# Turning the second layer's expert weights in beats 1 to 4 instead of ahead of the first score

## The chip, the cores and the metric

The kernel runs on one core of one Trainium2 chip. The metric is the device time of one execution in microseconds (us). The engines are TensorE (PE in the profile, with PEld for its weight loads), VectorE (DVE), ScalarE (ACT), GpSimd (POOL) and SyncE (SP), which here issues nearly all the transfers.

## The reference

The input x is 8 sequences of 512 tokens with 128 features. Everything is float32.

```
x = x + attention(layernorm(x))      # 16 heads of 8 features; Q, K, V and output projections 128x128, with biases
u = layernorm(x)
logits = u @ Wr.T + br               # 8 experts, the best 2 of each token, gates by softmax of the two
h = relu(u @ W1[e].T + b1[e])        # W1: 8 x 512 x 128
o = h @ W2[e].T + b2[e]              # W2: 8 x 128 x 512
x = x + layernorm_affine(u + sum over the 2 experts of gate * o)
```

## The kernel before

The work is in two blocks: attention with routing, then the experts. In the attention block each engine runs its own in-order program, and the programs are written as a loop over **beats** T, unrolled when the kernel is built, from -18 to 150. There are 16 beats per sequence (4 quads of heads times 4 tiles of 128 query tokens) and 8 sequences. A semaphore wait stands wherever one engine needs another's result.

In a beat T from 0 to 127, PE makes four score matmuls (`scores`, L810, one per head of a quad), each into one of three banks of `s_psum`, and DVE reduces each to a row maximum (`maxima`, L643). The score of number k (four per beat) waits until the reduction of number k-3 has freed its bank. Six beats later the same scores are made transposed (`scores_t`, L826), with the maximum added by rows of `qs` that the SHIFT task has brought in (mneg turned by PE at L848, copied by ACT at L512, sent by a DMA at L346). ACT takes their exponential into `pt` (L546), and two beats after that PE multiplies with the values (L896).

Between these, `early_tasks` places side tasks that share one bank, `side_psum`, and so one order. For sequence 0 the inputs are prepared in beats below 0. For sequence 1 they are: in beat 2 XT (four transposes of the normed input, L856, copied by ACT at L530), in beat 3 K and in beat 6 Q (a projection each, two instructions at L858; ACT takes the rounded part at L518, DVE the rest at L650, SP stores both to DRAM at L323). SHIFT of quad 0 is in beat 4. The first transposed score is in beat 6.

SP issues in beat -6 all loads of K and Q parts of sequence 0 (L334, L339), then the inputs of sequences 2 to 7 (L363).

The **expert weights** are 16 blocks of 128x512: eight of W1, eight of W2. They are loaded into `pt` (which the exponentials use only from beat 6 on; the program calls them w1raw and w2raw). A block is turned by four PE transposes (L929) into a bank of `st_psum`, block n into bank n mod 3. ACT copies it out (L589), rounded into `w1h` for W1, whole into `w2t` for W2. For W1, DVE also writes the remainder `w1l` (L714). PE waits before block n until block n-3 is copied, and before the very first transposed score until all 16 are (`if k == 0`). `expert_weights(T)` says which blocks belong to beat T. It is called at the end of the beat on PE, ACT and DVE.

Of the kernel before, what the change touches and what calls it, by code (L numbers as in the profile page):

```python
# [35 lines left out]
E = 8  # L36
# [81 lines left out]

def expert_weights(T):

    return range(2 * (T + 8), 2 * (T + 8) + 2) if -8 <= T < 0 else ()


def tiles(b, j=0, count=TILES):
# [44 lines left out]
def attention(nc, x, Wq, bq, Wk, bk, Wv, bv, Wo, bo, Wr, br, W1, b1, W2, beta, kept, sent, parts):  # L169
    xres, ident, fill = kept.xres, kept.ident, kept.fill  # L170
    with ExitStack() as ctx:
# [328 lines left out]
        def _(act):  # L500
# [31 lines left out]
            def beat(T):  # L532
# [51 lines left out]
                for n in expert_weights(T):  # L584
                    act.wait_ge(turned, n + 1)
                    src = weights_bank(n).rearrange("p (c d) -> p c d", c=FC)
                    dst = kept.w1h if n < E else kept.w2t
                    at = FC * (n % E)
                    nc.scalar.copy(dst[:, at:at + FC, :], src).then_inc(w_high, 1)  # L589
# [13 lines left out]
        def _(dve):  # L603
# [75 lines left out]
            def beat(T):  # L679
# [30 lines left out]
                for n in expert_weights(T):  # L710
                    if n < E:
                        dve.wait_ge(w_high, n + 1)
                        at = slice(FC * n, FC * n + FC)
                        nc.vector.tensor_tensor(kept.w1l[:, at, :], weights_bank(n).rearrange("p (c d) -> p c d", c=FC),  # L714
                                                kept.w1h[:, at, :].bitcast(F32), ALU.subtract).then_inc(w_low, 1)
# [65 lines left out]
        def _(pe):  # L781
# [118 lines left out]
            def beat(T):  # L900
# [18 lines left out]
                for n in expert_weights(T):  # L919
                    if n == 0:  # L920
                        pe.wait_ge(cols_ready, 1)
                    if n % E == 0:
                        pe.wait_ge((w1_loaded, w2_loaded)[n // E], 16)
                    if n >= ST_BANKS:
                        pe.wait_ge(w_high, n - ST_BANKS + 1)
                        pe.wait_ge(w_low, min(n - ST_BANKS + 1, E))
                    for c in range(FC):
                        src = w1raw[:, FC * n + c, :] if n < E else w2raw[:, n - E, P * c:P * c + P]
                        ins = nc.tensor.transpose(weights_bank(n)[:, P * c:P * c + P], src, ident[:])  # L929
                    ins.then_inc(turned, 1)  # L930
# [315 lines left out]
```

## Time and profile before

| | us |
|---|---|
| median of 3 runs | 753.96 |
| lowest, highest | 751.37, 755.16 |
| profiled execution | 752.29 |
| its span | 750.5 |
| PE busy | 609.3 (81%) |
| DVE busy | 489.0 (65%) |
| ACT busy | 447.4 (60%) |
| POOL busy | 242.6 (32%) |

The span is the profiled stretch of the program; 1.8 us of the execution's time lie around it. The attention block fills the time to about 530 us, the experts most of the rest. The change touches what lies between 29 and 56 us. TensorE runs at one of two clocks, 1.2 or 2.4 GHz; the profile's column of the granted clock gives it as 0.50 or 1.00. Before the first recorded switch that column reads 1.00 whatever the clock is, so there the durations of like instructions tell it.

### The profile page before, as it was taken

The page shows a single profiled execution, that of the slowest core. Times are in us where ns is not written, and L with a number is a line of the kernel's source. Part 1 is how long each engine was busy: PE and PEld are TensorE (multiplying, and loading weights), DVE is VectorE, ACT ScalarE, POOL GpSimd, SP SyncE. Part 2 cuts the span into 40 slices and gives each one's busy share as a digit, 9 for nine tenths or more (in the row PEclk, how much of TensorE's full clock was granted, in tenths as well). Part 3 has the DMA queues.
Part 4 walks back from the last instruction along what each step waited for, and adds up shares of the span by engine and source line. Part 5 has one row for each costly group of instructions (what it writes and reads, how often), then busy time and mean ns, then how long its engine had stood idle before and what let it go on. Part 6 is the DMA issues. An engine that isn't in the chain of part 4 may idle for free. (4 is left out here: it accounts for less than half of the span.)

```text
span 750.5 us, 13269 instructions
## 1 busy us (share of the span) xinstructions
PE 609.3 (81%) x3750; PEld 321.2 (43%) x3750; DVE 489.0 (65%) x1319; ACT 447.4 (60%) x945; POOL 242.6 (32%) x454
## 2 busy tenths in 40 slices
PE   2899999879988997987987998995229998999680
PEld 1633333323333432332332333332128988888530
DVE  3579989968967985985995887751204444444357
ACT  2718888867956965875885786683114444544333
POOL 5200101150240332214115005016425665555534
PEclk9959999989998998998998899899559999999976
DMA  7552122122122122022112211000121221221193
GB/s 219 195 153 66 44 69 83 49 67 74 37 85 72 33 84 84 26 65 89 49 47 70 65 45 48 6 0 30 50 83 54 65 66 56 69 66 57 47 238 98
DMA packets 54216, 54.47 MB, mean 73 GB/s; under 512 B 8286, under 2 KB 37514, under 8 KB 54164
## 3 DMA queue, kind: packets, MB, share of 16 engines
q1 hardware_dynamic: 48372, 44.19, 20.8%
q0 software_dynamic: 4416, 8.53, 3.2%
q10 hardware_dynamic: 1376, 1.13, 0.5%
q8 instruction: 24, 0.39, 0.2%
q14 instruction: 28, 0.23, 0.1%
HBM read 29.01 MB, written 24.81 MB: 72 GB/s over the span
## 5 line engine op out<-in xcount | busy, mean ns | idle before, releaser
L643 DVE TENSOR_REDUCE mneg<-s_psum 128x1 f32<-128x512 f32 x512 | 325.9, 684 | 89.5 <-PE s_psum L810 55.7
L546 ACT ACTIVATE pt<-st_psum 128x512 f32<-128x512 f32 x512 | 279.9, 598 | 93.3 <-PE st_psum L826 82.7
L826 PE MATMUL st_psum<-qs,ks 64*128 64x512 f32 x512 | 202.5, 471 | 24.8 <-ACT pt L546 19.4
L810 PE MATMUL s_psum<-ks,qs 64*128 64x512 f32 x512 | 208.3, 482 | 3.3 <-DVE mneg L643 2.1
L896 PE MATMUL pv_psum<-pt,vst 128*16 128x512 f32 x1024 | 142.8, 632 | 0.0
L810 PEld LDWEIGHTS s_psum<-ks,qs 64*128 64x128 f32 x512 | 84.4, 196 | 120.2 <-DVE mneg L643 94.9
L826 PEld LDWEIGHTS st_psum<-qs,ks 64*128 64x128 f32 x512 | 82.4, 193 | 69.1 <-ACT pt L546 52.7
L1099 ACT ACTIVATE hid<-h_psum,b1c 128x256 f32<-128x256 f32 x144 | 57.2, 474 | 71.2 <-PE h_psum L1204 69.3
L1062 POOL DMA_INDIRECT results<-res,goal_now x72 | 71.6, 994 | 33.7 <-issue 33.7
L1211 PE MATMUL y_psum<-w2t,hid 128*128 128x128 f32 x576 | 73.1, 280 | 0.0
L1211 PEld LDWEIGHTS y_psum<-w2t,hid 128*128 128x128 f32 x576 | 68.9, 194 | 0.9 <-issue 0.2
L490 POOL DMA_INDIRECT sent<-xrow,placeu x64 | 62.3, 973 | 18.4 <-issue 18.4
L1144 DVE COPY goal_now<-goals 128x1 uint32 x72 | 11.1, 154 | 64.2 <-DMA results<-res,goal_now 57.1
L461 POOL TENSOR_TENSOR vareps<-moments,eps 128x4 f32<-128x4 f32 x8 | 1.6, 200 | 149.2 <-DVE moments L726 149.1
L1202 PE MATMUL h_psum<-xh,w1h 128*128 128x256 f32 x144 | 44.0, 306 | 2.5 <-DVE xl L1120 2.3
L1190 PE MATMUL x_psum<-ident,lot 128*128 128x128 f32 x74 | 16.5, 306 | 33.2 <-DMA lot<-sent 33.1
L1204 PE MATMUL h_psum<-xh,w1l 128*128 128x256 f32 x144 | 41.0, 285 | 0.0
L1203 PE MATMUL h_psum<-xl,w1h 128*128 128x256 f32 x144 | 41.0, 285 | 0.0
L896 PEld LDWEIGHTS pv_psum<-pt,vst 128*16 128x16 f32 x1024 | 17.0, 95 | 39.3 <-ACT pt L546 22.6
L538 ACT COPY pvs<-pv_psum 128x512 f32<-128x512 f32 x32 | 18.8, 589 | 25.1 <-remote 14.4
L1091 ACT CAST xh<-x_psum 128x256 fp32r<-128x256 f32 x37 | 13.9, 376 | 33.1 <-PE x_psum L1190 32.3
L428 POOL TENSOR_TENSOR start<-fill,zero_e 128x8 f32<-128x8 f32 x8 | 1.6, 204 | 89.0 <-DVE counts L691 89.0
(164 smaller groups left out, 711.3 us busy)
## 6 DMA issues: line engine op xcount, KB each, us to landing
parts<-high SPq DMA_DIRECT2D x32, 256.0 KB, 3.0
ks<-parts SPq DMA_DIRECT2D x128, 48.0 KB
qs<-parts SPq DMA_DIRECT2D x128, 48.0 KB
lot<-sent SPq DMA_DIRECT2D x37, 132.0 KB
parts<-low SPq DMA_DIRECT2D x16, 256.0 KB, 3.1
got<-results SPq DMA_DIRECT2D x16, 256.0 KB, 5.1
xres<-in_L_attn_x_dram SPq DMA_DIRECT2D x8, 256.0 KB, 3.6
pt<-in_L_ffn_W_dram SPq DMA_DIRECT2D x1, 2048.0 KB, 14.5
```

What stands on the lines that cost most here:

```text
L490: nc.gpsimd.indirect_dma_start(out=sent, out_offset=bass.IndirectOffsetOnAxis(ap=placeu[:, j, k:k + 1], axis=0), in_=xrow[:, k, j, :], in_ ...
L546: nc.scalar.activation(pt[:, n % PT_SLOTS, (g + 2) % 4, :], st_psum[:, k % ST_BANKS, :], ACT.Exp, scale=SCALE).then_inc(exp_done, 1)
L643: nc.vector.tensor_reduce(mneg[:, (n // 4) % 2, at:at + 1], s_psum[:, k % S_BANKS, :], AX_X, ALU.max, negate=True).then_inc(max_done, 1)
L810: mm(s_psum[:, k % S_BANKS, :], qs[rows, c, P * (n % 4):P * (n % 4) + P], ks[rows, c, g, :], start=True, stop=True).then_inc(s_made, 1)
L826: mm(st_psum[:, k % ST_BANKS, :], ks[rows, c, g, P * (n % 4):P * (n % 4) + P], qs[rows, c, :], start=True, stop=True).then_inc(st_made, 1)
L896: ins = mm(pv_psum[32 * g:32 * g + 16, 0, :], vst[:, b % 2, n % 4, 4 * (q % QUADS) + g, :], pt[:, n % PT_SLOTS, g, :], start=(n % 4 == 0), ...
L1062: nc.gpsimd.indirect_dma_start(out=results, out_offset=bass.IndirectOffsetOnAxis(ap=goal_now[:, h:h + 1], axis=0), in_=res[:, h, :], in_of ...
L1099: nc.scalar.activation(hid[:, f, :], h_psum[:, f, 0:SLOTS], ACT.Relu, bias=b1c[:, FC * e + f:FC * e + f + 1]).then_inc(relu_act, 1)
L1202: mm(dst, w1h[:, k, :], xh[:], start=True, stop=False)
L1203: mm(dst, w1h[:, k, :], xl[:], start=False, stop=False)
L1204: mm(dst, w1l[:, k, :], xh[:], start=False, stop=True).then_inc(h_made, 1)
L1211: ins = mm(y_psum[:, h, 0:D], hid[:, f, P * h:P * h + P], w2t[:, FC * e + f, :], start=(f == 0), stop=(f == FC - 1))
```

## The change

One function is changed. The eight blocks of W1 stay in beats -8 to -5, two each. The eight blocks of W2 move from beats -4 to -1 into beats 1 to 4, two each, on PE and on ACT. On DVE nothing moves, since it has no work for W2.

```diff
 def expert_weights(T):
 
-    return range(2 * (T + 8), 2 * (T + 8) + 2) if -8 <= T < 0 else ()
+    if -8 <= T < -4:
+        return range(2 * (T + 8), 2 * (T + 8) + 2)
+    return range(E + 2 * (T - 1), E + 2 * (T - 1) + 2) if 1 <= T < 5 else ()
```

The lines below the change stand two lines lower in the changed file (L929 is L931 there, L810 is L812, and so on). On PE, the place from the last blocks of W1 to the first transposed score, before the change:

```order
L929 MATMUL st_psum<-ident,pt 128x128 [waits w_low,w_high]
L929 MATMUL st_psum<-ident,pt 128x128 x3
L810 MATMUL s_psum<-ks,qs 128x512 [waits kq_in0]
L810 MATMUL s_psum<-ks,qs 128x512 x2
L810 MATMUL s_psum<-ks,qs 128x512 [waits max_done] x7
L856 MATMUL side_psum<-ident,xn 128x128 [waits xn_done,side_done]
L856 MATMUL side_psum<-ident,xn 128x128 x3
L810 MATMUL s_psum<-ks,qs 128x512 [waits max_done] x4
L858 MATMUL side_psum<-xt,wt 128x512 [waits side_done]
L810 MATMUL s_psum<-ks,qs 128x512 [waits max_done] x2
```

And the beginning of the same place after it (beats 0 to 3):

```order
L812 MATMUL s_psum<-ks,qs 128x512 [waits kq_in0]
L812 MATMUL s_psum<-ks,qs 128x512 x2
L812 MATMUL s_psum<-ks,qs 128x512 [waits max_done] x5
L931 MATMUL st_psum<-ident,pt 128x128 [waits w_low,w_high,w2_loaded]
L931 MATMUL st_psum<-ident,pt 128x128 x3
L931 MATMUL st_psum<-ident,pt 128x128 [waits w_low,w_high]
L931 MATMUL st_psum<-ident,pt 128x128 x3
L812 MATMUL s_psum<-ks,qs 128x512 [waits max_done] x2
L858 MATMUL side_psum<-ident,xn 128x128 [waits xn_done,side_done]
L858 MATMUL side_psum<-ident,xn 128x128 x3
L812 MATMUL s_psum<-ks,qs 128x512 [waits max_done] x2
```

The 32 transposes of W2 no longer stand ahead of the first score; eight of them follow the fourth score of each of the beats 1 to 4. On ACT, before:

```order
L589 CAST w1h<-st_psum 128x512 [waits turned] x8
L589 COPY w2t<-st_psum 128x512 [waits turned] x8
L564 ACTIVATE xn<-xres,shift,rstd 128x128 [waits shift_done]
L564 ACTIVATE xn<-xres,shift,rstd 128x128 x3
L530 COPY xt<-side_psum 128x512 [waits side_made]
L518 ACTIVATE high<-side_psum,bcols 128x512 [waits k_stored,side_made]
L512 CAST shift_rows<-side_psum 16x128 [waits side_made]
```

and after:

```order
L591 CAST w1h<-st_psum 128x512 [waits turned] x8
L566 ACTIVATE xn<-xres,shift,rstd 128x128 [waits shift_done]
L566 ACTIVATE xn<-xres,shift,rstd 128x128 x3
L591 COPY w2t<-st_psum 128x512 [waits turned] x2
L532 COPY xt<-side_psum 128x512 [waits side_made]
L591 COPY w2t<-st_psum 128x512 [waits turned] x2
L520 ACTIVATE high<-side_psum,bcols 128x512 [waits k_stored,side_made]
L591 COPY w2t<-st_psum 128x512 [waits turned] x2
L514 CAST shift_rows<-side_psum 16x128 [waits side_made]
L591 COPY w2t<-st_psum 128x512 [waits turned] x2
```

The eight copies now stand in pairs around the copies of XT, K and SHIFT, and the norm of sequence 1 is no longer behind them.

## Rows read from the trace of the kernel before

**Rows 1.** PE in order of time (start, duration, instruction, idle before), beats -8 to 6.

```profile
22.30 2.82 PE L929 MATMUL st_psum<-ident,pt 128*128 128x128 f32 x12 [0.53 <-DVE wrt L634]
25.36 4.06 PE L929 MATMUL st_psum<-ident,pt 128*128 128x128 f32 x20 [0.24 <-DVE w1l L714]
29.65 4.20 PE L929 MATMUL st_psum<-ident,pt 128*128 128x128 f32 x32 [0.23 <-DVE w1l L714]
33.78 0.73 PE L810 MATMUL s_psum<-ks,qs 64*128 64x512 f32 x3
...
39.37 1.11 PE L856 MATMUL side_psum<-ident,xn 128*128 128x128 f32 x4
...
42.71 2.07 PE L858 MATMUL side_psum<-xt,wt 128*128 128x512 f32 x2
...
51.93 0.79 PE L826 MATMUL st_psum<-qs,ks 64*128 64x512 f32 x1
...
53.08 2.07 PE L858 MATMUL side_psum<-xt,wt 128*128 128x512 f32 x2
```

**Rows 2.** DVE in order of time, from the last remainders of W1 to beat 6.

```profile
30.69 0.86 DVE L608 BATCH_NORM_STATS2 stats<-xres 128x6 f32<-128x128 f32 x4
31.59 0.38 DVE L613 BATCH_NORM_AGGREGATE moments<-stats 128x2 f32<-128x6 f32 x4
34.31 6.07 DVE L643 TENSOR_REDUCE mneg<-s_psum 128x1 f32<-128x512 f32 x10 [2.35 <-PE s_psum L810]
41.24 2.48 DVE L643 TENSOR_REDUCE mneg<-s_psum 128x1 f32<-128x512 f32 x4 [0.86 <-PE s_psum L810]
45.54 1.29 DVE L643 TENSOR_REDUCE mneg<-s_psum 128x1 f32<-128x512 f32 x2 [1.82 <-PE s_psum L810]
46.75 0.74 DVE L650 SCALAR_TENSOR_TENSOR low<-side_psum,bcols,high 128x512 fp32r<-128x512 f32 x1
47.41 6.15 DVE L643 TENSOR_REDUCE mneg<-s_psum 128x1 f32<-128x512 f32 x10
55.91 1.29 DVE L643 TENSOR_REDUCE mneg<-s_psum 128x1 f32<-128x512 f32 x2 [2.36 <-PE s_psum L810]
```

**Rows 3.** Stretches: length, busy us (count) of PE, PEld, DVE, ACT, POOL, granted clock, DMA share, GB/s.

```profile
38.00:38.50 0.50, 0.45 (x1) 0.18 (x1) 0.50 (x1) 0.00 (x0) 0.00 (x0) 1.00 0.32 98
38.50:39.00 0.50, 0.40 (x2) 0.28 (x1) 0.50 (x2) 0.00 (x0) 0.00 (x0) 0.60 0.37 127
...
46.50:47.00 0.50, 0.50 (x1) 0.07 (x1) 0.50 (x2) 0.00 (x0) 0.00 (x0) 0.50 1.31 313
47.00:47.50 0.50, 0.08 (x1) 0.00 (x0) 0.50 (x2) 0.00 (x0) 0.00 (x0) 0.50 0.43 103
...
48.50:49.00 0.50, 0.50 (x3) 0.27 (x1) 0.50 (x2) 0.00 (x0) 0.00 (x0) 0.50 0.43 98
...
51.00:51.50 0.50, 0.50 (x2) 0.28 (x1) 0.50 (x2) 0.00 (x0) 0.00 (x0) 0.50 0.57 205
51.50:52.00 0.50, 0.50 (x3) 0.07 (x3) 0.50 (x2) 0.00 (x0) 0.00 (x0) 0.50 0.00 0
...
55.50:56.00 0.50, 0.50 (x6) 0.27 (x4) 0.09 (x1) 0.12 (x1) 0.00 (x0) 0.83 0.00 0
```

**Rows 4.** L929's transposes, 22 to 27.5 us: duration ns min/median/max, first and last start.

```profile
L929 PE MATMUL st_psum<-ident,pt x22: 421/421/476, 22.3 to 27.3; 128*128 128x128 f32 x22
```

**Rows 5.** L929's transposes from 29 to 34 us.

```profile
L929 PE MATMUL st_psum<-ident,pt x36: 272/273/328, 28.8 to 33.6; 128*128 128x128 f32 x36
```

**Rows 6.** SP's issues in order of time.

```profile
24.73 1.67 SPq L339 DMA_DIRECT2D ks<-parts  x4
26.51 1.52 SPq L339 DMA_DIRECT2D qs<-parts  x4
...
40.38 3.29 SPq L363 DMA_DIRECT2D xres<-in_L_attn_x_dram  x6
```

**Rows 7.** Transfers of the first 60 us: size, median us from issue to landing.

```profile
parts<-high SPq DMA_DIRECT2D x6, 256.0 KB, 3.3
...
xn<-in_L_ffn_b_dram SPq DMA_DIRECT2D x1, 16.0 KB, 2.4
```

**Rows 8.** PE in order of time, a later projection in the fast clock.

```profile
91.47 0.50 PE L826 MATMUL st_psum<-qs,ks 64*128 64x512 f32 x1
...
92.13 1.13 PE L858 MATMUL side_psum<-xt,wt 128*128 128x512 f32 x2
93.19 0.50 PE L810 MATMUL s_psum<-ks,qs 64*128 64x512 f32 x1
```

**Rows 9.** Groups by line, 34 to 56 us: busy us, mean ns, idle before, released by.

```profile
L643 DVE TENSOR_REDUCE mneg<-s_psum 128x1 f32<-128x512 f32 x27 | 16.7, 681 | 7.4 <-PE s_psum L810 7.4
...
L826 PEld LDWEIGHTS st_psum<-qs,ks 64*128 64x128 f32 x5 | 1.2, 285 | 1.9 <-issue 1.5 <-DMA qs<-shift_rows 0.4
```

**Rows 10.** DVE after that projection.

```profile
93.76 1.29 DVE L643 TENSOR_REDUCE mneg<-s_psum 128x1 f32<-128x512 f32 x2 [0.47 <-PE s_psum L810]
```

## The prediction

> **What bounds the kernel now.** I read the page first, then PE, DVE, ACT and SP in order of time over the first 80 us, then the granted clock in short stretches. The page says that the attention block keeps PE, DVE and ACT all busy. The change moves no work out of the kernel, so it can only gain where an engine that sets the pace stands idle, and lose where it adds to that engine's line. Those places lie between 29 and 56 us. From beat 7 on the beats follow one another by events alone; nothing there is tied to a fixed time, so I take a lead that is won by then as kept to the end.
>
> The reader should see three things. First, PE turns W2 from 29.65 to 33.8 us and makes the first score at 33.78 [rows 1], while DVE has finished all it had to do at 31.97 and waits 2.35 us for that score [rows 2]. Here the moved work stands on the path. Second, from the first reduction to beat 6 DVE goes on without a pause except in three places: 0.86 us behind XT, 1.82 us behind the K projection, 2.36 us behind the Q projection and the first transposed score [rows 2]. Third, TensorE is in the slow clock for the last two: it fell at about 38.6 and rose at about 55.7 us [rows 3]. The transposes tell that it was also slow at the start: they took 421 ns up to 27.3 us and 273 ns from 28.8 us on [rows 4, 5].
>
> I follow the lead of the changed kernel, the time by which the same reduction on DVE starts earlier than before. Reductions are counted from 0, four per beat, 0.607 us each (6.07 / 10 [rows 2]).
>
> **Removed: the wait ahead of the first score.** DVE's work up to 31.97 is unchanged. PE has the last W1 block done at about 29.4 (25.36 + 4.06 [rows 1]). The first score then needs the first loads of K and Q. Their last issue ends at 28.03 (26.51 + 1.52 [rows 6]). The trace has no landing for them; a smaller transfer landed 2.4 us after its issue and a larger one 3.3 us [rows 7], so they are there between 30.4 and 31.3. With the 0.53 us from a first score's start to its reduction (34.31 - 33.78), DVE could start between 30.9 and 31.9. Both ends are before 31.97, so DVE's own work decides: a lead of 34.31 - 31.97 = 2.34 us. The cover at the late end is only 0.1 us. If the loads come 1 us later than that, the lead is 0.9 us less.
>
> **Moved: eight transposes into each of beats 1 to 4.** In the fast clock 32 of them take 4.20 us, 0.131 each; in the slow clock the first twelve take 2.82 us, or (2.82 - 0.42) / 11 = 0.218 each [rows 1, 4]. Two blocks cost PE 1.05 us fast or 1.75 us slow. What hides them is the supply of three filled banks, 1.8 us of reductions, less the time to make the next score (0.5 fast, 0.8 slow). The fast case fits in; the slow one does not, by about 1 us. So the clock decides the rest.
>
> Before, the clock fell after PE had gone over from dense transposes to scores alone, paced by DVE at 0.61 us. In the changed kernel that stretch starts at about 30 instead of 33.8, so I take the clock as slow by beat 1. Then: score 7 waits for reduction 4 to end, at 31.97 + 5 x 0.607 = 35.0; with its 0.45 us the transposes run from 35.5 to 37.25. Score 8 is ready 0.79 us later, at 38.0. DVE ran dry at 36.8. Before, reduction 8 started at 34.31 + 8 x 0.607 = 39.2, so the lead is 1.2 us. XT follows score 9 at 38.1 and takes 1.11 us, and reduction 10 starts at 39.9 against 41.24 [rows 2]: lead 1.3.
>
> From 35.0 on PE has no pause at all: score, transposes, two scores, XT, two scores, and beat 2's transposes (40.0 to 41.75). I take it that this brings the fast clock back at about 42, before the K projection. What speaks for it is the start: between 22.3 and 27.3 us PE did nothing but these transposes, and by 28.8 it was fast [rows 1, 4, 5]. The Trainium skill, in "TensorE: Matmul & The Clock Gate", section "Part 4: PE-mode transpose", says the contrary, that transposes do not engage the full clock and do not count as busy in the same way. The trace differs, 421 ns and then 273 ns with only transposes between. By the page the clock would stay low through beats 1 to 4, which is the last rival below.
>
> With the fast clock the K projection takes 1.13 us [rows 8] for 2.07 [rows 1]. It runs from about 42.5 to 43.6, reduction 14 starts at 44.05 (45.54 before), the K remainder ends at 45.95 and reduction 16 starts there (47.41 before): lead 1.5. The transposes of beats 3 and 4 take 1.05 us each behind three filled banks and cost nothing. If that cover is gone they cost what rival 3 and 4 give.
>
> **The copies on ACT.** Two copies a beat, 1.1 us, where ACT is otherwise nearly idle up to beat 6. Behind them stand the XT copy, the K part and the SHIFT copy. Beat 1's pair ends at 37.9 and XT is made at 39.2, so nothing waits. Beat 2's pair ends at about 42.4, before the K projection does. The norm of sequence 1 comes about 1 us earlier on ACT. All of this I cost at nothing, at most 0.3 us. The wait of the first transposed score for all 16 blocks is met at least 3 us before.
>
> **Beat 6.** The first transposed score waits for the SHIFT rows, a transfer that SP issues behind the three stores of K. From the end of the K remainder (47.41) to that score (51.93) it was 4.5 us [rows 1, 2], and the score's last wait was for those rows [rows 9]. So it comes at 45.95 + 4.5 = 50.4, and the lead is still 1.5. From it to reduction 26 it was 55.91 - 51.93 = 3.98 us, of which 2.07 are the Q projection in the slow clock. In the fast clock the same pieces are 0.66 from a transposed score to the projection and 1.63 from the projection to the reduction behind it (92.13 - 91.47 and 93.76 - 92.13 [rows 8, 10]), together 2.3. Reduction 26 starts at 52.7 for 55.91: lead 3.2. This is the sum: 2.3 won at the start, 0.8 lost net up to beat 4, 1.7 won at Q. Against the profiled execution it gives 752.29 - 3.2 = 749.1, against the median 753.96 - 3.2 = 750.8. The profiled execution lies low in the three runs, so I weight the median more and say **750.5**.
>
> **Rivals.**
>
> 1. *The clock stays or comes back sooner.* If it is fast before the beat 2 transposes, or never falls, the K remainder would end 0.9 to 1.8 us sooner still. But then something else is late: the six input loads, issued from 40.38 on, keep the DMA engines full until 47.0 [rows 3, 6], and the stores of K and the SHIFT rows stand behind them. The stores' data moved from about 48.5 to 51.4 [rows 3]. The first transposed score is then at about 49.9, a lead of 2.0, and with 1.7 at Q it is 3.7 to 4.0: about 750.1 to 750.3 on the median, 748.5 on the profiled execution. For it: XT and transposes are dense work. Against it: PE's sparse scores are longer alone at the start. The Trainium skill, "DMA: Bandwidth & Descriptors", section "Queues, rings and completion order", says that a ring's descriptors are consumed in order, which is the reason for this queueing; no row here separates the rings.
> 2. *The clock comes back late*, in beat 3 or 4, behind the K projection. Before, one K projection at 42.7 did not bring it back, though PE was busy [rows 1, 3]. Then the lead at K is about 0.1 us (39.9 + 2.8 to the projection's start, against 42.71), 0 to 0.3 at the first transposed score, and 1.7 from Q: 1.9 us, 752.1 on the median.
> 3. *The lead is lost at the start or later*: the first loads come late (up to 1 us), or a later stretch of slow clock moves against it. The gain is then 0 to 2 us, 753.
> 4. *The slow clock lasts through beats 1 to 5 (slower).* Then PE sets the pace. K runs 42.6 to 44.7 as before, two blocks of transposes from 45.4 to 47.2 make reduction 16 start at 47.9 (47.41 before), beat 4's run from 49.4 to 51.1, score 20 is ready at 51.8 when DVE ran dry at 50.4, and the first transposed score stands behind five scores at 53.4 instead of 51.93: 1.5 us later, and no gain at Q. The time would be 755.5 on the median, 753.8 on the profiled execution. It decides from the point where two or more of the four pairs are turned in the slow clock behind the K projection. Against it: PE would have no pause at all in all these beats.
>
> **Numbers.** Forecast 0.42, rival 1 0.23, rival 2 0.17, rival 3 0.10, rival 4 0.08. The three runs are spread by 3.8 us, 0.5%, which is about what can be told from no change. A gain over 0.5% is 3.77 us; only rival 1 reaches it, and the forecast by the scatter of medians: 0.34 in all. Slower by over 0.5% needs rival 4 and scatter: 0.05. The rest, 0.61, is the same. The range from 747.0 to 754.6 holds rivals 1 to 3 with 2 us of scatter; the forecast alone would be 748.5 to 752.
>
> **What would show it.** DVE's first reduction at 32.0, not 34.3 (if later, the loads). Transposes of beat 1 at 421 ns and of beats 3 and 4 at 273 ns; the clock slow from about 35 and fast again before the K projection, which then takes 1.1 us. The K remainder ends near 46, the first transposed score is near 50.4, its idle time still put down to the SHIFT rows, reduction 26 near 52.7. The total of DVE's idle time up to there falls from 7.4 us [rows 9] to about 4. I am wrong if K or Q still takes 2.07 us, if the first transposed score comes after 51.9, or if the lead at beat 7 is not found again in the last reduction of the attention block.

## The result and the profile after

The changed kernel is slower by about half a percent, which is small but clear of the scatter: a median of 757.26 us over 18 runs (749.83 to 759.10) against 751.76 us over 18 runs of the kernel before (748.38 to 755.19), ratio 1.0052 with a 95% interval of 1.0033 to 1.0071 (the two medians alone give 1.0073). The profiled execution took 756.26 us with a span of 754.5 (750.5 before). The forecast was 750.5, from a lead of 3.2 us. The range ended at 754.6, so the time lies outside it.

The ratios leave out executions over 1.5% above the fastest of the same kernel; for two kernels below that removes many, so their medians over all executions are given too.

The beginning came as forecast. DVE in order of time (start, duration, instruction, idle before it), which answers to [rows 2]:

```profile
31.45 4.84 DVE L645 TENSOR_REDUCE mneg<-s_psum 128x1 f32<-128x512 f32 x8
37.99 1.29 DVE L645 TENSOR_REDUCE mneg<-s_psum 128x1 f32<-128x512 f32 x2 [1.71 <-PE s_psum L812]
40.19 1.29 DVE L645 TENSOR_REDUCE mneg<-s_psum 128x1 f32<-128x512 f32 x2 [0.91 <-PE s_psum L812]
43.23 1.29 DVE L645 TENSOR_REDUCE mneg<-s_psum 128x1 f32<-128x512 f32 x2 [1.76 <-PE s_psum L812]
46.39 1.29 DVE L645 TENSOR_REDUCE mneg<-s_psum 128x1 f32<-128x512 f32 x2 [1.86 <-PE s_psum L812]
...
53.95 3.68 DVE L645 TENSOR_REDUCE mneg<-s_psum 128x1 f32<-128x512 f32 x6 [1.76 <-PE s_psum L812]
59.48 1.29 DVE L645 TENSOR_REDUCE mneg<-s_psum 128x1 f32<-128x512 f32 x2 [1.86 <-PE s_psum L812]
```

The first reduction starts at 31.45 instead of 34.31, with no wait in front of it: a lead of 2.9 us. Reduction 8 is at 37.99 (38.0 forecast), reduction 10 at 40.19 (39.9). Then the lead goes. Reduction 12 is at 43.23, reduction 14 at 46.39 against 45.54 before, and reduction 26 at 59.48 against 55.91: 3.6 us late.

PE in order of time, which answers to [rows 1], shows why:

```profile
29.51 0.73 PE L812 MATMUL s_psum<-ks,qs 64*128 64x512 f32 x3 [0.52 <-DMA qs<-parts]
32.16 3.18 PE L812 MATMUL s_psum<-ks,qs 64*128 64x512 f32 x5 [1.92 <-DVE mneg L645]
35.27 1.97 PE L931 MATMUL st_psum<-ident,pt 128*128 128x128 f32 x8
37.16 1.22 PE L812 MATMUL s_psum<-ks,qs 64*128 64x512 f32 x2
38.31 1.12 PE L858 MATMUL side_psum<-ident,xn 128*128 128x128 f32 x4
...
40.51 1.97 PE L931 MATMUL st_psum<-ident,pt 128*128 128x128 f32 x8
42.41 1.22 PE L812 MATMUL s_psum<-ks,qs 64*128 64x512 f32 x2
43.55 2.07 PE L860 MATMUL side_psum<-xt,wt 128*128 128x512 f32 x2
...
55.39 0.76 PE L828 MATMUL st_psum<-qs,ks 64*128 64x512 f32 x1
```

The loads were there at 29.5. All four pairs of blocks take 1.97 us, and K, and later Q, take 2.07. From 35.27 to 54.3 us PE has no idle time at all: PE sets the pace and DVE waits. The next idle time, 0.36 us, stands ahead of a score at 54.69. The granted clock, by stretch (columns as in [rows 3]):

```profile
30.00:32.00 2.00, 0.24 (x3) 0.00 (x0) 1.97 (x10) 0.00 (x0) 0.31 (x2) 1.00 0.44 123
32.00:34.00 2.00, 1.75 (x4) 0.80 (x4) 2.00 (x5) 0.64 (x2) 1.25 (x3) 0.68 0.26 82
34.00:60.00 26.00, 25.64 (x70) 13.85 (x69) 14.87 (x24) 8.93 (x18) 1.27 (x1) 0.50 0.44 125
60.00:62.00 2.00, 1.22 (x8) 0.70 (x6) 2.00 (x5) 2.00 (x5) 0.00 (x0) 1.00 0.00 0
```

PE was idle for nearly two microseconds from 30.24 on, since it had made three scores and DVE freed the first bank only at 32.1. PE went on at 32.16, and the clock fell within the next stretch, at about 32.7 (0.68 in the mean), and stayed at 1.2 GHz for all of 34 to 60 us, though PE was busy for 25.64 of these 26. Before, it was slow from 38.6 to 55.7 [rows 3]. The totals by line from 29 to 61 us (columns as in [rows 9]) say the same: DVE's reductions waited 11.1 us for PE's scores (7.4 before, in the stretch of [rows 9]), and the 32 transposes average 426 ns.

```profile
L645 DVE TENSOR_REDUCE mneg<-s_psum 128x1 f32<-128x512 f32 x28 | 17.5, 681 | 11.1 <-PE s_psum L812 11.1
...
L931 PE MATMUL st_psum<-ident,pt 128*128 128x128 f32 x32 | 7.9, 426 | 0.0
```

Compared at the same instruction of later batches, the profiled execution stays 3.6 to 5.0 us late to the end of the attention block, and ends 4.0 us late.

### The profile page after: what moved, and what is told of

The parts are those of the page before. It is cut to its first block and busy times, and to the rows that moved or that the text cites. A ratio compares the mean times of both kernels' runs of the same rounds, so it can differ in the third digit from the quotient of the medians.

```text
span 754.5 us, 13269 instructions
## 1 busy us (share of the span) xinstructions
PE 612.5 (81%) x3750; PEld 323.2 (43%) x3750; DVE 488.8 (65%) x1319; ACT 447.6 (59%) x945; POOL 242.3 (32%) x454
## 3 DMA queue, kind: packets, MB, share of 16 engines
q10 hardware_dynamic: 1376, 1.13, 0.5%
## 5 line engine op out<-in xcount | busy, mean ns | idle before, releaser
L812 PE MATMUL s_psum<-ks,qs 64*128 64x512 f32 x512 | 209.5, 484 | 4.1 <-DVE mneg L645 2.7
L812 PEld LDWEIGHTS s_psum<-ks,qs 64*128 64x128 f32 x512 | 84.9, 198 | 120.1 <-DVE mneg L645 90.3
L1146 DVE COPY goal_now<-goals 128x1 uint32 x72 | 11.1, 154 | 63.3 <-DMA results<-res,goal_now 52.7
L1192 PE MATMUL x_psum<-ident,lot 128*128 128x128 f32 x74 | 16.6, 307 | 33.9 <-DMA lot<-sent 33.4
L1093 ACT CAST xh<-x_psum 128x256 fp32r<-128x256 f32 x37 | 13.8, 374 | 33.7 <-PE x_psum L1192 32.6
```

Of the source, the lines that this page charges most:

```text
L812: mm(s_psum[:, k % S_BANKS, :], qs[rows, c, P * (n % 4):P * (n % 4) + P], ks[rows, c, g, :], start=True, stop=True).then_inc(s_made, 1)
```

## The experiments

Each kernel is the changed one or the one before, as said, with the edit shown; "..." marks lines left out. Each was timed beside the kernel before, whose median was 753.28, 747.87 or 747.55 us in the three sets, so a kernel is compared within its own set. A gain is called shown only where the interval of the ratio stays below 1 and the median over all executions agrees. "Reduction 26" is the first one behind the Q projection in beat 6: at 55.91 us before and at 59.48 in the changed kernel.

**The transposes left out.** Changed kernel; the result lacks W2's turned form.

```diff
-                    act.wait_ge(turned, n + 1)
+                    act.wait_ge(turned, min(n + 1, E))
...
+                    if n >= E:
+                        continue
                     if n == 0:
                         pe.wait_ge(cols_ready, 1)
```

> The changed kernel with the 32 PE transposes of W2 left out (ACT's eight copies stay and copy what is in the banks, so W2's turned form is not computed). Theory A (the transposes in beats 1 to 4, all in the slow clock, are the whole loss): the first reduction stays at about 31.5 us, the clock still falls at about 33 and stays low through K and Q, and reduction 26 starts at 52.8 to 53.5 us instead of 59.5 (before 55.9); the time is 2.5 to 3 us under before, ratio 0.996 to 0.997. Theory B (the early start itself costs, by loads or stores that come into each other's way): reduction 26 comes at 55 or later, ratio 0.999 to 1.002.

Measured: 752.10 us against 753.28, ratio 0.9982 (0.9959 to 1.0004). Reduction 26 starts at 54.15, a lead of 1.8. The clock fell at 31.8, in the same idle time, and rose at 55.7. So the early start is real, and the transposes in the slow clock are the difference of 5.3 us at reduction 26. The forecast of 52.8 to 53.5 was too early: the first transposed score waited 0.6 us for the SHIFT rows, and the first reduction came at 31.85. For the whole execution no gain is shown, since the interval holds 1; see the end of this section.

**Ordinary matmuls against the identity in place of the transposes of W2.** Changed kernel.

```diff
-                        ins = nc.tensor.transpose(weights_bank(n)[:, P * c:P * c + P], src, ident[:])
+                        if n < E:
+                            ins = nc.tensor.transpose(weights_bank(n)[:, P * c:P * c + P], src, ident[:])
+                        else:
+                            ins = mm(weights_bank(n)[:, P * c:P * c + P], src, ident[:], start=True, stop=True)
```

> The changed kernel with the eight W2 blocks of beats 1 to 4 turned by ordinary matmuls against the identity instead of transposes: same count and shape, but more array time each (an ordinary 128x128 one has about twice the passes of a transpose). Theory A with the page's rule (transposes do not hold or bring the fast clock, ordinary matmuls do): the clock rises in beat 1, 2 or 3, before 46 us; K then takes 1.1 us and reduction 26 starts at 54 to 57.5, ratio 0.998 to 1.003, in spite of the dearer instruction. Theory C (the kind of instruction is the same to the clock, it stays low because PE's work in these beats is too thin): the pairs cost about 3.4 us each in the slow clock, reduction 26 starts at 64 or later, ratio 1.010 or more.

Measured: 753.44 us against 753.28, ratio 1.0015 (0.9983 to 1.0046). PE in order of time:

```profile
35.52 3.78 PE L934 MATMUL st_psum<-ident,pt 128*128 128x128 f32 x16
...
42.57 3.78 PE L934 MATMUL st_psum<-ident,pt 128*128 128x128 f32 x16
46.28 1.21 PE L812 MATMUL s_psum<-ks,qs 64*128 64x512 f32 x2
47.42 1.12 PE L860 MATMUL side_psum<-xt,wt 128*128 128x512 f32 x2
48.48 0.73 PE L812 MATMUL s_psum<-ks,qs 64*128 64x512 f32 x2
49.14 2.05 PE L934 MATMUL st_psum<-ident,pt 128*128 128x128 f32 x16
```

A pair of blocks is now 16 instructions instead of 8 and takes 3.78 us instead of 1.97 in the slow clock, yet the clock came back at 47.4 us, in the place where with transposes it did not for 13 us more. It came later than expected (46), and reduction 26 is at 59.33, later than expected (54 to 57.5), as the two dear pairs had been paid by then. Ordinary matmuls do here what the transposes did not. They also keep the array busy twice as long, so kind and amount aren't told apart by this run.

**Four blocks ahead, one in each of beats 1 to 4.** All by transposes. The edit is written against the changed kernel.

```diff
-    if -8 <= T < -4:
+    if -8 <= T < -2:
         return range(2 * (T + 8), 2 * (T + 8) + 2)
-    return range(E + 2 * (T - 1), E + 2 * (T - 1) + 2) if 1 <= T < 5 else ()
+    return range(12 + (T - 1), 13 + (T - 1)) if 1 <= T < 5 else ()
```

> Four W2 blocks ahead of the first score (beats -4 and -3), one in each of beats 1 to 4. PE stood idle for about 2 us between the first scores in the changed kernel, so both theories expect the first reduction at 31.5 to 32.0. Theory A: the four blocks left cost 0.9 us each in the slow clock, mostly hidden (three banks give 1.8 us less 0.8); reduction 26 starts at 54 to 56, ratio 0.997 to 1.000. Theory B: no gain over before, 1.000 to 1.003.

Measured: 750.72 us against 753.28, ratio 0.9973 (0.9949 to 0.9997). The first reduction is at 31.76 (31.45 in the changed kernel) after a wait of 0.48 us for its score, so four blocks ahead cost at most half a microsecond: they fill most of the time in which PE would have waited for the loads and for DVE. The clock fell at 35.7, in beat 1. From the end of the transposes at 31.3 PE made scores alone, with no idle time over 0.55 us, and the four transposes of beat 1 had begun only at 35.33. Reduction 26 is at 55.80, level with the kernel before, so the 0.3% of the whole time did not come from these beats.

**The clock held in the kernel before by an added projection.** Its result is not read.

```diff
+                if 0 <= T < 6:
+                    pe.wait_ge(w_high, 2 * E)
+                    mm(st_psum[:, 1, :], wt[:, 0, :], xt[:, 0], start=True, stop=True)
```

> The kernel before with one more ordinary 128x128 by 128x512 projection at the end of each of beats 0 to 5, whose result nothing reads. It measures what the slow clock of 38.6 to 55.7 us costs the kernel before. If ordinary matmuls hold the fast clock (theory A with the page's rule): the clock does not fall before beat 7, the added projections take 1.1 us each and are hidden, K and Q take 1.13 instead of 2.07, reduction 26 starts at 52.5 to 54 instead of 55.9, ratio 0.996 to 0.998. If the clock falls all the same (theory C): the added ones take 2.07 us each, PE sets the pace, reduction 26 starts at 61 or later, ratio 1.006 or more.

Measured: 749.08 us against 753.28, ratio 0.9936 (0.9907 to 0.9966). More work and a shorter time. PE's stretch, and DVE at Q:

```profile
34.00:60.00 26.00, 23.12 (x83) 9.60 (x83) 22.86 (x38) 9.81 (x22) 1.27 (x1) 1.00 0.43 124
```

```profile
53.71 1.29 DVE L643 TENSOR_REDUCE mneg<-s_psum 128x1 f32<-128x512 f32 x2 [1.03 <-PE s_psum L810]
```

The clock does not fall from 34 to 60 us (granted 1.00). Between the first reduction and reduction 26 DVE waits 3.0 us in all, where it waited 5.0 (0.86, 1.82 and 2.36 us in [rows 2]). Reduction 26 is 2.2 us earlier; 0.67 us of that was there at the first reduction (33.64 against 34.31), ahead of all added work. So the slow clock costs the kernel before about 2 us up to this point, and the twin that follows, whose first reduction is level, gives the cleaner number.

**The same with eight transposes in place of the projection.** The twin of the last, in the kernel before.

```diff
+                if 0 <= T < 6:
+                    pe.wait_ge(w_high, 2 * E)
+                    for i in range(8):
+                        nc.tensor.transpose(st_psum[:, 1, P * (i % 4):P * (i % 4) + P], xt[:, 0, P * (i % 4):P * (i % 4) + P],
+                                            ident[:])
```

> The kernel before with eight more transposes at the end of each of beats 0 to 5 (about the time of one projection in the fast clock), whose result nothing reads. It is the twin of the run that added one projection there and kept the fast clock. If transposes do not count for the clock: it falls between 35 and 39 us as before, the added ones then take 1.75 to 2.0 us a beat, and reduction 26 starts at 60 to 63 us; ratio 1.004 to 1.010. If any dense work counts: the clock stays fast, reduction 26 starts at 53.5 to 54, ratio 0.993 to 0.998.

Measured: 744.48 us against 747.87, ratio 0.9953 (0.9922 to 0.9984). The 48 added transposes, by duration (ns min/median/max), and the clock over 38 to 56 us:

```profile
L921 PE MATMUL st_psum<-ident,xt x48: 272/273/331, 35.5 to 51.0; 128*128 128x128 f32 x48
```

```profile
38.00:56.00 18.00, 16.34 (x80) 9.31 (x80) 15.74 (x26) 4.94 (x10) 0.00 (x0) 1.00 0.54 159
```

The clock does not fall with transposes either. The first reduction is at 34.30, as before, and reduction 26 at 53.71, so the whole lead of 2.2 us comes from the stretch between. That both twins have reduction 26 at 53.71 is in part chance: the projections' kernel started 0.67 us earlier, and then waited 0.24 us for the SHIFT rows, which PE used at 51.4 us in both.

**64 transposes without a pause ahead of the first score.** Kernel before; one execution.

```diff
+                if T == -1:
+                    pe.wait_ge(w_high, 2 * E - 2)
+                    for i in range(64):
+                        nc.tensor.transpose(...)
```

> The kernel before with 64 more transposes, without a pause, ahead of the first score (8.4 us in the fast clock). In the kernel before, the clock rose at about 28 us with only transposes since 22.3, which speaks against the rule that transposes do not count. If dense transposes hold the clock: they all take about 273 ns, the clock falls only after they end at about 42. If they do not: it falls amid them, before 39 us, and the rest take 421 ns. The first reduction comes at 42 to 46 us and the time is 8 to 12 us longer either way.

Measured: 753.70 us, one execution, 5.8 us over the median of the kernel before where 8 to 12 was expected; the 64 transposes took 7.2 us and not 8.4, and the first reduction came at 40.79, ahead of the 42 to 46 expected. All 64 took 272 to 326 ns. The clock fell at 46.1 us, nearly 6 us after they ended, with scores and, just ahead of the fall, the four transposes of XT in between, and no idle time over 0.55 us. The Trainium skill, in "TensorE: Matmul & The Clock Gate", section "Part 4: PE-mode transpose", has it that transposes do not engage the full clock. These two runs disagree for an array that is already fast. In the slow clock of the changed kernel, eight transposes a beat among scores did not bring it back, which agrees; at the start of the kernel before it rose with transposes alone [rows 4, 5], which does not.

**The changed kernel with the clock held.** Two projections in the gap of beat 0, half of one in each of beats 1 to 4, one in beat 5; the transposes where the change has them.

```diff
+                if T == 0:
+                    pe.wait_ge(side_done, SIDE["Q", 0] + 1)
+                    for _ in range(2):
+                        mm(side_psum[:, 0, :], wt[:, 0, :], xt[:, 0], start=True, stop=True)
                 scores(T, 3)
...
+                if 1 <= T < 6:
...
+                    cols = 256 if T < 5 else 512
+                    mm(st_psum[:, (n0 - 1) % ST_BANKS, 0:cols], wt[:, 0, :], xt[:, 0, 0:cols], start=True, stop=True)
```

> The changed kernel with the clock held by ordinary matmuls whose results nothing reads: two projections between the third and fourth score of beat 0, where PE stood idle, half a projection in each of beats 1 to 4, one in beat 5. The W2 transposes stay where the change put them. Theory A (the slow clock, not the place, made the move dear): the clock stays fast, each pair of blocks takes 1.05 us, PE has about 2.9 us of work a beat for 2.43 of DVE, and reduction 26 starts at 52.5 to 54.5 instead of 59.5; ratio 0.991 to 0.997. Theory P (the place costs in either clock, by waits on the copies or by the order behind the scores): reduction 26 at 57 or later, ratio 1.000 or more.

Measured: 747.10 us against 747.87, ratio 0.9981 (0.9954 to 1.0007). Each pair took 1.04 us, K 1.12, and the K remainder ended at 44.1, a lead of 3.4 over the kernel before. But the first transposed score started at 51.88 and had waited 1.67 us for the SHIFT rows. The clock fell soon after this wait, at 53.3, and reduction 26 came at 54.72, just behind the 54.5 expected. For the whole execution no gain over the kernel before is shown.

**Only the gap of beat 0 filled.** Changed kernel with the first of these two edits alone.

```diff
+                if T == 0:
+                    pe.wait_ge(side_done, SIDE["Q", 0] + 1)
+                    for _ in range(2):
+                        mm(side_psum[:, 0, :], wt[:, 0, :], xt[:, 0], start=True, stop=True)
                 scores(T, 3)
```

> The changed kernel with one edit: two projections whose result nothing reads stand between the third and fourth score of beat 0, where PE was idle for 1.9 us. Nothing is added in beats 1 to 6. Theory D, formed from the runs so far: transposes do hold the fast clock, but do not bring it back when the array is in the slow one; the changed kernel loses because the clock falls in the gap that the change opens ahead of beat 1. Then here the clock stays fast at least through beats 1 to 4, the four pairs take 1.05 us each, K takes 1.1, and reduction 26 starts at 52.5 to 55 instead of 59.5; ratio to before 0.993 to 0.999. Against it, theory E (transposes amid scores do not hold it, the added work of the other run in beats 1 to 4 did): the clock falls before 42 us and reduction 26 is at 57 or later, ratio 1.001 or more.

Measured: 746.97 us against 747.55, ratio 0.9979 (0.9941 to 1.0017). PE in order of time, and the clock:

```profile
30.13 1.98 PE L915 MATMUL side_psum<-xt,wt 128*128 128x512 f32 x4
32.61 2.89 PE L812 MATMUL s_psum<-ks,qs 64*128 64x512 f32 x5 [0.49 <-DVE mneg L645]
35.43 1.09 PE L935 MATMUL st_psum<-ident,pt 128*128 128x128 f32 x8
...
40.05 1.12 PE L860 MATMUL side_psum<-xt,wt 128*128 128x512 f32 x2
...
50.63 0.49 PE L828 MATMUL st_psum<-qs,ks 64*128 64x512 f32 x1 [2.58 <-DMA qs<-shift_rows]
```

```profile
32.50:47.00 14.50, 13.44 (x60) 7.51 (x60) 13.19 (x23) 7.47 (x15) 2.48 (x4) 1.00 0.59 165
```

This is the run that names the cause. Nothing was added in beats 1 to 6, and yet the clock stayed fast, every pair took 1.09 us, and reduction 26 moved from 59.48 to 54.19. The clock fell only at 51.2, after PE's wait of 2.58 us for the SHIFT rows, so Q still took 2.08. The change lost because the clock was slow from ahead of beat 1 on, and two projections in the gap are enough to prevent it. Against the changed kernel, timed in the same set, the medians are 746.97 and 751.55 us; against the kernel before no gain is shown.

What this run does not tell apart is the idle time from the lack of dense work, for the two projections end both. In the changed kernel 6.3 us lie between the last transpose of W1 (29.0) and the first of W2 (35.27), with scores alone and 1.92 us of idle time. In three kernels without such idle time the clock fell all the same, 4.4 to 5.8 us after the last dense transposes: 31.3 to 35.7 with four blocks ahead, 33.9 to 38.6 before, 40.3 to 46.1 with 64 transposes. So it may well have fallen ahead of beat 1 without the idle time too. No run leaves the gap out and keeps the scores alone.

**The gap filled with work that is needed.** Four blocks ahead, two in beat 0, two in beat 1; nothing added.

```diff
-    if -8 <= T < -4:
+    if -8 <= T < -2:
         return range(2 * (T + 8), 2 * (T + 8) + 2)
-    return range(E + 2 * (T - 1), E + 2 * (T - 1) + 2) if 1 <= T < 5 else ()
+    return range(12 + 2 * T, 14 + 2 * T) if 0 <= T < 2 else ()
```

> No added work: four W2 blocks ahead of the first score, two at the end of beat 0, two at the end of beat 1, all by transposes. It fills the gap of beat 0 with work that has to be done anyway. Theory D: first reduction at 31.7, all transposes in the fast clock (1.05 us a pair), the clock falls later, at 38 to 42 us when scores are alone, as in the kernel before; K and Q take 2.07 and reduction 26 starts at 53 to 54; ratio 0.995 to 0.998. Theory E: the clock falls at about 35 as in the run with half moved, reduction 26 at 55 to 56, ratio 0.997 to 1.000.

Measured: ratio 0.9947 (0.9906 to 0.9988), from 8 of 12 executions; over all of them the median is 747.73 against 747.55, so no gain is shown. In its trace, of an execution of 750.00 us, the first reduction is at 31.75, the pairs take 1.1 us, and the K projection is still fast (39.63, 1.13 us); the clock fell at 45.7, later than the 38 to 42 expected, amid scores alone. The first transposed score is at 50.11 after 2.51 us of wait for the SHIFT rows, and reduction 26 at 54.12, a lead of 1.8.

**Both edits together.** Four blocks ahead by transposes; one block in each of beats 1 to 4 by ordinary matmuls; one unread projection in beats 0 and 5.

```diff
-    if -8 <= T < -4:
+    if -8 <= T < -2:
...
+    return range(12 + (T - 1), 13 + (T - 1)) if 1 <= T < 5 else ()
...
+                        if n < E + 4:
...
+                            ins = mm(weights_bank(n)[:, P * c:P * c + P], src, ident[:], start=True, stop=True)
...
+                if T in (0, 5):
+                    pe.wait_ge(w_high, 12 if T == 0 else 2 * E)
+                    mm(st_psum[:, 2 if T == 0 else 0, :], wt[:, 0, :], xt[:, 0], start=True, stop=True)
```

> Made from the two edits that paid: four W2 blocks turned by transposes ahead of the first score, where PE has nothing else; the other four one per beat in beats 1 to 4, turned by ordinary matmuls against the identity; and one projection with an unread result in beats 0 and 5. Theory A with the rule on transposes: the clock does not fall before beat 7, the first reduction starts at 31.5 to 31.9 and reduction 26 at 51.5 to 52.8, against 53.7 with the projections alone and 55.8 with the half move alone; ratio to before 0.989 to 0.994. Theory C: one ordinary block a beat is too thin, the clock falls at 35 to 38 and reduction 26 is at 55 to 58, ratio 0.998 to 1.003.

Measured: 742.77 us against 747.87, ratio 0.9924 (0.9892 to 0.9957). The K remainder ended at 43.9, but the first transposed score:

```profile
51.68 0.49 PE L828 MATMUL st_psum<-qs,ks 64*128 64x512 f32 x1 [2.37 <-DMA qs<-shift_rows]
```

It is hardly earlier than the 51.93 of [rows 1]. The clock fell at 52.8, after this wait, where it was expected to hold to beat 7, and reduction 26 is at 54.76, where 51.5 to 52.8 was expected. The gain over the kernel before is shown, but at 5.1 us of the medians it is larger than the lead of 1.15 us at reduction 26.

**The input loads issued behind the SHIFT rows.** The last kernel with one edit on SP: the loads of sequences 2 to 7 and of beta move from beat -6 to beat 5.

```diff
+                if T == 5:
                     for b in range(2, B):
                         sp.dma_start(xres[:, TILES * b:TILES * b + TILES, :], x_tiles[:, b]).then_inc(x_loaded, 16)
...
```

> The version with half ahead, ordinary matmuls and two projections, and on SP one edit: the six input loads and beta are issued in beat 5 instead of beat -6. There the first transposed score stood at 51.7 us and waited 2.4 us for the SHIFT rows, although the K remainder had ended at 43.9. If the wait is due to those loads ahead in the queue, the first transposed score comes at 48.5 to 49.5 and reduction 26 at 50.5 to 51.5, 2 to 4 us earlier than there; ratio to before 0.987 to 0.991. If it is the issue and the latency of SHIFT's own transfer, nothing changes: 0.991 to 0.994.

Measured: ratio 0.9845 (0.9790 to 0.9900), from 5 of 12 executions; over all, 742.56 us against 747.55, or 0.993. PE and DVE:

```profile
49.21 0.50 PE L829 MATMUL st_psum<-qs,ks 64*128 64x512 f32 x1
```

```profile
51.49 1.29 DVE L646 TENSOR_REDUCE mneg<-s_psum 128x1 f32<-128x512 f32 x2 [0.46 <-PE s_psum L813]
```

The score comes 2.5 us earlier and waits for nothing, and reduction 26 is 4.4 us ahead of the kernel before. So the loads held the SHIFT rows up. They did it in two ways, as SP's issues show, first with the loads ahead of the stores and then with the loads behind SHIFT:

```profile
41.37 3.40 SPq L365 DMA_DIRECT2D xres<-in_L_attn_x_dram  x6
44.81 0.51 SPq L366 DMA_DIRECT2D beta<-in_L_ffn_beta_dram  x1
45.78 1.22 SPq L325 DMA_DIRECT2D parts<-high  x2
...
47.69 0.60 SPq L348 DMA_DIRECT2D qs<-shift_rows  x1
```

```profile
44.30 1.22 SPq L325 DMA_DIRECT2D parts<-high  x2
...
46.22 0.60 SPq L348 DMA_DIRECT2D qs<-shift_rows  x1
```

With the loads ahead, SP was still issuing them and beta when the K remainder ended at 43.9, and the SHIFT rows were issued 3.8 us after that; with the loads behind, 1.9 us after it (44.3 to 46.22). That part, 1.9 us, is SP's own time. The rest is the transfer: 3.4 us from the end of SHIFT's issue to the score that waited for it (48.29 to 51.68), at most 2.4 with the loads behind (46.82 to 49.21).

This version beats the kernel before, by 5 us of the medians. It is not shown to be faster than the version it was made from: 742.56 us here and 742.77 there, in spite of 3.3 us more of lead at reduction 26.

**The changed kernel again**, for a second trace.

> The changed kernel itself once more, for a second trace. Its times spread from 750 to 759 us, so the clock may not take the same course in every execution. Theory D: in an execution near 757 the clock falls before beat 1's transposes and reduction 26 starts at 58 to 60; in one near 750 the fall comes later or a rise before K, and reduction 26 is at 53 to 56. Ratio to before 1.004 to 1.008.

Measured: 751.55 us against 747.55, ratio 1.0042 (1.0012 to 1.0071). The clock took the same course (down at 32.0, up at 59.3), and reduction 26 is at 59.16. The idle time was 1.60 us here and the clock fell within 0.2 us after its end (31.84). The traced execution took 755.39; none near 749 was traced, so where the lower times of this kernel come from is open.

**What stays open behind beat 7.** A lead at reduction 26 isn't kept exactly, although the prediction took it as kept. The run without transposes had still 1.7 us at reduction 144 and 0.2 at reduction 148, where its trace has a slow stretch at 147 to 151 us that the kernel before lacks. The run with only the gap filled had 1.7 at reduction 26 and 9.6 at the last reduction of the attention block, the one with eight added transposes a beat 2.2 and 0.4. Besides, a trace is one execution, and not always a typical one: those of the run with only the gap filled and of the changed kernel with the clock held are the fastest of 12, those of the two runs with work added to the kernel before the slowest of 10. The medians follow the leads at reduction 26 only to about 4 us, more than the effect of this change, so what is shown of the cause is shown up to reduction 26.

## Why the prediction was wrong

- **Removed wait.** Right: 2.9 us instead of 2.34, since W1's remainders also ended 0.4 us earlier in this execution. The loads were there at 29.5, earlier than the 30.4 to 31.3 of the estimate.
- **The clock slow by beat 1.** Right: it fell at 32.7. I took the fall as given by scores alone and put no price on it. The run with the gap filled shows that it need not have fallen before beat 6. The idle time ahead of the fourth score followed from my own numbers: three scores made by 31.1 to 32.0, the next only after DVE's first reduction at 32.6.
- **"I take it that this brings the fast clock back at about 42, before the K projection."** This is the step that failed. The clock did not come back before 60 us, though PE was busy with scores, transposes and two projections for 25.64 of the 26 us from 34 on. The start of the kernel, on which I leaned, was transposes alone, without scores between; that this is what made the difference is not shown. Two traces of the changed kernel agree. All that the forecast took from the fast clock went with this step: 0.9 us at K, 1.7 at Q, and the hidden pairs of beats 3 and 4.
- **Rival 4, the slow clock through beats 1 to 5,** is what happened, with a chance of 0.08. Its mechanism was right, its size short: 3.6 us instead of 1.5. A pair of blocks takes PE 1.9 us from start to the next instruction where I had 1.75 (35.27 to 37.16), and a pair of slow scores 1.15 where I had about 0.85 (37.16 to 38.31). With this the first transposed score is at 55.39 and not at 53.4. That Q brings no gain was right: from that score to reduction 26 it was 4.1 us, 4.0 before.
- **The Trainium skill's section on PE-mode transpose** spoke for rival 4. It came out right on the time, though not on its reason: the fast clock held with transposes in two runs. I had dismissed it on one stretch of trace, where it should have had a larger chance.
- **Rival 1's cap** was right in kind and too mild: with the clock held, the SHIFT rows behind the input loads set the first transposed score at 50.1 to 51.9, not 49.9. The run with the loads moved shows it, and that part of the delay is SP's issuing and not the queue.
- **A lead kept to the end.** The profiled execution was 3.6 us late at reduction 26 and between 3.6 and 5.0 behind it, which is near enough here. The experiments show that it does not hold to better than about 4 us.
- **The copies on ACT** cost nothing, as said.

## What to carry to other kernels

When a change takes dense work off TensorE ahead of a loop that another engine paces, look at what TensorE does between the dense stretches that are left. Here scores alone and 1.9 us of idle time, 6.3 us together, cost the fast clock for the next 27, and that was more than the whole loss at reduction 26 (5.3 us won back, 3.6 lost). Look first for work that has to be done anyway: four of the eight blocks cost at most half a microsecond ahead of the first score, and with the other four in beats 0 and 1 the clock stayed fast through the K projection. That gave a lead of 1.8 us in its trace, though no shorter median. And when a wait is shortened, look at what is issued and queued ahead of the next transfer: here 1.5 MB of loads that nobody needed yet held up 8 KB that everybody waited for.

## What the runs showed of the hardware that was not expected

- Eight transposes a beat among scores, added to the kernel before, left the clock at 1.00 as one projection a beat did. In the changed kernel, which was slow when they came, eight a beat in four beats did not bring it back: it stayed at 0.50 from 34 to 60 us. Ordinary matmuls in their place, twice the instructions and twice the time, were followed by its return at 47.4, 12 us after the first of them.
- The kernel before with six projections added that nobody reads was faster: 0.9936 (0.9907 to 0.9966). About 2 us of it is seen up to reduction 26; where the rest comes from is open.
